# A graph convolution with experts on one core: three more batches give four columns to TensorE, deviations run ahead of block counts, and VectorE turns the experts' tiles

## The chip, the cores and the metric

The kernel runs on one core of a Trainium2 chip. Five engines run their own instruction streams and meet through semaphores: TensorE (PE, matrix products), VectorE (DVE), ScalarE (ACT), GpSimd (POOL, here mostly indirect transfers) and SyncE (SP, which issues most other transfers). The metric is the device time of one execution in microseconds; the time before is the median of three runs, 3089.98 us (3088.39 to 3091.4).

## The reference

Two graph-attention convolutions (GAT) over 6250 nodes and 206250 edges, self-loops included, then a layer of eight experts of which each node uses two. Cut to what matters:

```python
def _gat_conv(x, W, att_src, att_dst, bias, src, dst):      # 8 heads of 16 channels
    xw = (x @ W).reshape(N, H, CPH)
    a_s, a_d = (xw * att_src).sum(-1), (xw * att_dst).sum(-1)
    e = leaky_relu(a_s[src] + a_d[dst], 0.2)
    p = exp(e - segment_max(e, dst)[dst])
    alpha = p / segment_sum(p, dst)[dst]
    return segment_sum(xw[src] * alpha[:, :, None], dst).reshape(N, H * CPH) + bias

def gnn(x, edge_index, ...):
    h0 = _gat_conv(x, W0, ..., row, col)
    h1 = _gat_conv(x, W1, ..., row[col], col[col])          # and the loops
    return _layernorm(concat([h0, h1], -1) + x) * gamma + beta

def ffn(x, Wg, bg, W1, b1, W2, b2):
    top_w, top_i = top_k(x @ Wg + bg, 2)                    # softmax over the two
    return sum(w_e * (gelu(x @ W1[e] + b1[e]) @ W2[e] + b2[e] for e of 8))

x = x + gnn(_layernorm(x), ...)
out = x + ffn(_layernorm(x), ...)
```

## The kernel before

The edges are sorted by target. The program goes through four stages.

The prologue (to about 237 us) loads the nodes in 49 tiles of 128 (NT), in seven groups of seven (GRP). VectorE takes the layer norm's statistics, ScalarE the deviations (`deviation(g)`, L988), VectorE normalises (`scales`, `normalise`, from L1469), TensorE multiplies each tile with both W, and ScalarE copies the products out (`rows(t)`, L998); SP stores them as rows of tables in memory (L613), between 26 stores of 496 KB that clear another array (L607). At the same time the first edge of each node is searched: ScalarE compares block starts (`search_signs`), GpSimd fetches one block of targets per tile by an indirect transfer (`fetch_blocks(n)`, L834, seven per group), and ScalarE counts in it (`within(t)`, L1006). A block's buffer is used again 14 blocks later, so a fetch of groups 2 and up waits for a count (`block_counted`). ScalarE's order is written out: seven counts `within(0)` to `within(6)`, then `deviation(0)`, then steps t in which `rows(t)` stands with the counts that `counted_at(t)` lists. GpSimd then scatters scores into the array that was cleared (`scatter_scores`, L842) and gathers the rows of the first 49 edge columns.

The batch stage (to about 2006 us) goes over 51 batches of up to 31 columns of 128 chunks of edges. GpSimd fetches each column's rows with one indirect gather (`gather(b)`, L881, L886), into one of three slots; it waits for an index list and for the stores of the batch that had the slot three batches before. VectorE (`scan_batch`, from L1685) and ScalarE compute attention weights and running sums along the chunks, and SP stores them (L665). In batches PE0 to 49 four columns (PEC) are not gathered: TensorE picks their rows by one-hot products with a table that VectorE and ScalarE have split in parts (`split_table`, from batch SPLIT_AT on). For these, codes of the columns' sources are computed (`code_columns`), stored to memory by one transfer (L710) and read back for each batch (`fetch_codes`, L650). All index lists, codes and stores go through the one queue of SP, in program order. In the first batches VectorE and ScalarE also normalise the nodes again, a group per batch in batches 1 to 7 (`normalise_again`, L1130; `add_biases`, L1924), through one buffer `norm_again`, and SP stores the group (L697, L698). The sums that continue from one chunk to the next are corrected in two rounds: `run_maxima`, `run_sums`, `fix_maxima`, `fix_sums` on VectorE, `carry_exps`, `fix_exps` on ScalarE, and on GpSimd an indirect fetch and an indirect store of rows (L895, L901).

A third stage combines both convolutions per node and computes the router's choice. Each node's normalised row, with its number, its two weights and its first expert behind it (260 words), is scattered to `placed` in the order of experts.

The expert stage (about 2303 to 3078 us) goes over 105 tiles of 128 rows (SLOTS). SP loads a tile from a row number that it reads from `reg` (`tile_after`, L794, L799). TensorE turns it in two transposes (`turn`, L1390, L1392) into PSUM, VectorE copies it to `xsT` (`turned`, L2177). TensorE multiplies it with the expert's W1 (`up`, L1395, L1401), ScalarE applies gelu (L1247), TensorE multiplies with W2 (`down`, L1405, L1407). VectorE copies the expert's W1 in two halves to `w1_cur` (`take_weights`, L2187), each once TensorE has used the half before; it computes the rows' weights (`weights_of`, L2193 to L2201) and weighs the answer (L2228, L2230), and GpSimd adds it to `out` by an indirect transfer (L960). Tiles use two buffers. The load of tile t + 2 is issued when the tile t + 1 has been turned and the row weights of tile t are computed (`row_ids_copied`).

## Time and profile before

| | us |
|---|---|
| median of three runs | 3089.98 (3088.39 to 3091.4) |
| the profiled execution | 3084.84 |
| its span | 3083.1 |
| GpSimd busy in the span | 1897.6 (62%) |
| TensorE busy | 2068.2 (67%) |
| VectorE busy | 2168.5 (70%) |
| ScalarE busy | 1588.3 (52%) |
| first batch's first gather to the last one's end | 236.6 to 2005.8 |

The busy shares are means over stages with different limits, so no engine looks like the bound in them. The profile is read stage by stage: by the chain of work that ended last, by the costliest groups of instructions with the idle time ahead of them and what ended it, by the busy times of a stretch, and by the timelines of single engines, where a number in brackets is the idle time before an instruction and behind it what it waited for. "issue" there is time in which the engine waited for nothing that the profile shows.

### The profile page before, as it was taken

How to read it: one execution, taken by the hardware profiler on the slowest of the kernel's cores; microseconds unless marked ns; L12 is line 12 of the kernel's file. 1: busy time of each engine (PE TensorE's matmuls, PEld its weight loads, DVE VectorE, ACT ScalarE, POOL GpSimd, SP SyncE). 2: the span in 40 equal slices, each digit the busy share in tenths (PEclk: the TensorE clock that was granted, in tenths of full speed). 3: DMA queues.
4: the chain of work that ended last, by engine and by line, in shares of the span. 5: the costliest groups of instructions: out<-in, count | busy, mean ns of one | idle time of the engine just before them, and what ended most of it. 6: DMA issues, size and time to landing. Idle time of an engine off the chain costs nothing.

```text
span 3083.1 us, 41470 instructions
## 1 busy us (share of the span) xinstructions
PE 2068.2 (67%) x11476; PEld 1955.4 (63%) x11477; DVE 2168.5 (70%) x4427; ACT 1588.3 (52%) x2552; POOL 1897.6 (62%) x1880
## 2 busy tenths in 40 slices
PE   3800000058888788788878878503549999999998
PEld 1500000058888788788878878503439999999997
DVE  5668767678788878878888887888844444444443
ACT  4523333267777777777777777524423333333332
POOL 4777777777777777777777777777762222222222
PEclk9855555579899898989989898855559999999999
DMA  9445459944444444444444444475672222222222
GB/s 343 131 123 145 169 168 204 155 124 126 139 147 126 126 160 126 126 138 148 126 126 160 126 126 140 138 247 185 228 242 35 36 36 38 36 36 38 36 36 31
DMA packets 216756, 394.75 MB, mean 128 GB/s; under 512 B 80877, under 2 KB 169266, under 8 KB 210146
## 3 DMA queue, kind: packets, MB, share of 16 engines
q1 hardware_dynamic: 141169, 247.04, 24.1%
q0 software_dynamic: 74384, 146.42, 21.2%
q10 hardware_dynamic: 1120, 0.52, 0.1%
q14 instruction: 71, 0.57, 0.1%
q8 instruction: 12, 0.20, 0.0%
HBM read 202.05 MB, written 191.79 MB: 128 GB/s over the span
## 4 chain that ended last, share of the span: by engine, by line
POOL 46%; PE 26%; issue 16%; DVE 6%; DMA 2%; SPq 2%; ACT 1%; DVEq 1%; POOLq 0%; ACTq 0%
POOL AR L886 43%; PE ps L1401 12%; PE ps L1407 12%; DMA tables<-AR 1%; PE ps L1274 1%; POOL room L923 1%; PE ps L1392 1%; DVE group_stats L1968 1%; ACT AR L1207 1%; SPq L607 1%; DVE AR L1672 1%; POOL placed L951 1%; SPq L591 1%; POOL adstart L846 0%; DVE AR L2092 0%
## 5 line engine op out<-in xcount | busy, mean ns | idle before, releaser
L886 POOL DMA_INDIRECT AR<-tables,idx x1403 | 1336.9, 953 | 429.6 <-issue 427.3
L1303 PE MATMUL ps<-table_parts,onehot 128*128 128x408 f32 (+1 forms) x4080 | 881.3, 379 | 322.0 <-DVE AR L1784 164.2
L1303 PEld LDWEIGHTS ps<-table_parts,onehot 128*128 128x128 f32 x4080 | 836.3, 215 | 353.8 <-ACT onehot L1163 192.4
L1088 ACT COPY AR<-AR 128x1984 f32<-128x1984 f32 (+3 forms) x110 | 401.5, 3650 | 353.1 <-DVE AR L1719 310.4
L960 POOL DMA_INDIRECT out<-AR,idb x105 | 185.3, 1765 | 592.3 <-issue 558.3
L1719 DVE TENSOR_TENSOR_SCAN AR<-ps,AR 128x512 f32<-128x512 f32 x404 | 454.1, 1195 | 0.0
L1401 PEld LDWEIGHTS ps<-AR 128*128 128x128 f32 x3360 | 393.2, 193 | 6.6 <-DVE AR L2187 1.3
L1401 PE MATMUL ps<-AR 128*128 128x128 f32 x3360 | 393.8, 276 | 0.9 <-DVE AR L2187 0.9
L1712 DVE TENSOR_TENSOR AR<-AR,ps 128x3968 f32<-128x3968 f32 (+1 forms) x51 | 356.4, 6988 | 0.0
L2187 DVE COPY AR<-AR 128x1024 f32 x210 | 151.6, 722 | 208.2 <-PE ps L1401 206.7
L1303 PE MATMUL ps<-table_parts,onehot_dve 128*128 128x408 f32 (+1 forms) x1360 | 272.3, 343 | 0.0
L1247 ACT ACTIVATE AR<-ps,bcur 128x128 f32<-128x128 f32 x424 | 121.1, 369 | 258.5 <-PE ps L1401 258.5
L1163 ACT ACTIVATE onehot<-onehot 128x1536 fp32r<-128x1536 f32 (+1 forms) x160 | 250.6, 1566 | 5.1
L1247 ACT ACTIVATE room<-ps,bcur 128x128 f32<-128x128 f32 x416 | 118.9, 368 | 253.6 <-PE ps L1401 253.4
L1303 PEld LDWEIGHTS ps<-table_parts,onehot_dve 128*128 128x128 f32 x1360 | 246.8, 188 | 0.2
L1691 DVE TENSOR_TENSOR AR<-AR,ps 128x248 f32<-128x248 f32 (+1 forms) x51 | 29.4, 576 | 232.5 <-DMA AR<-tables,idx 232.5
L1407 PE MATMUL ps<-AR 128*128 x848 | 191.9, 379 | 1.3 <-DVE AR L2230 1.3
L1335 PE MATMUL ps<-ident,sml 128*128 128x128 f32 x6 | 2.4, 501 | 281.2 <-DVE sml L1866 281.2
L1407 PE MATMUL ps<-AR,room 128*128 x832 | 188.2, 379 | 0.0
L1159 ACT ACTIVATE onehot<-AR,minus_code 128x384 fp32r<-128x384 f16 x340 | 180.6, 609 | 5.0 <-DVE table_parts L1809 5.0
L1335 PEld LDWEIGHTS ps<-ident,sml 128*128 128x128 f32 x6 | 1.5, 312 | 282.1 <-DVE sml L1866 282.1
L1159 ACT ACTIVATE onehot<-room,minus_code 128x384 fp32r<-128x384 f16 x340 | 180.4, 605 | 0.0
(350 smaller groups left out, 2808.4 us busy)
## 6 DMA issues: line engine op xcount, KB each, us to landing
state<-AR SPq DMA_DIRECT2D x50, 2232.0 KB, 9.6
AR<-tables,idx POOLq DMA_INDIRECT x1452
AR<-in_L_ffn_W SPq DMA_DIRECT2D x16, 1024.0 KB, 10.0
AR<-placed SPq DMA_DIRECT2D x105, 130.0 KB, 2.1
adstart<-room SPq DMA_DIRECT2D x26, 496.0 KB, 13.6
AR<-adstart SPq DMA_DIRECT2D x50, 248.0 KB, 4.0
tables<-AR SPq DMA_DIRECT2D x49, 136.0 KB, 2.2
room<-tables SPq DMA_DIRECT2D x14, 476.0 KB, 4.6
```

The source lines that it names most:

```text
L886: pool.indirect_dma_start(out=G[s][:, j, 0:ROWT], out_offset=None, in_=table_rows, in_offset=bass.IndirectOffsetOnAxis(ap=idx[:, s, j:j + ...
L960: pool.indirect_dma_start(out=out, out_offset=bass.IndirectOffsetOnAxis(ap=idb[:, s, :], axis=0), in_=ys[:, s, :], in_offset=None, bounds_ ...
L1088: return S.copy(to.rearrange("p j (h c) -> p j h c", h=HD)[:, :, :, a:z], of[:, :, 1:n + 1].rearrange("p (c h) j -> p j h c", h=HD)[:, :, ...
L1159: last = S.activation(onehot[:, a, :], column_codes[b % 2][:, 0:ACT_C * P], ACT.Abs, bias=minus_code[:, v:v + 1])
L1163: S.activation(onehot[:, first:end, :], onehot[:, first:end, :], ACT.Relu, bias=1.0, scale=-1.0).then_inc(marked_by_act, 1)
L1247: last = S.activation(hsT[s][:, m, :], ps[2 * s + h][:, (m % 4) * P:(m % 4 + 1) * P], ACT.Gelu, bias=bcur[:, s, m:m + 1])
L1303: return T.matmul(bank[:, 0:z], mark, table_parts[:, k, v * w:v * w + z], start=(a == 0 and k == 0), stop=(a == LEV - 1 and k == PARTS - 1))
L1401: mm = T.matmul(ps[2 * s + h][:, m * P:(m + 1) * P], w1_cur[:, k, (h * 4 + m) * P:(h * 4 + m + 1) * P], xsT[:, s, k, :], start=(k == 0), s ...
L1407: mm = T.matmul(ps[5][:, 0:D], hsT[s][:, m, :], AR[:, bass.ds(e * (MH * D) + (NEX * KD * HID + m * D), D)], start=(m == 0), stop=(m == MH ...
L1712: V.tensor_tensor(TS[:, 0:F, js].rearrange("p (c h) j -> p c h j", h=HD), rows_in[:, :, 0:F].rearrange("p j (h c) -> p c h j", h=HD), bc(W ...
L1719: V.tensor_tensor_scan(T2[:, i * step:(i + 1) * step], decays(w), T2[:, i * step:(i + 1) * step], 0.0, ALU.mult, ALU.add).then_inc(entry_u ...
L2187: V.tensor_copy(w1_cur[:, :, h * 512:(h + 1) * 512], w1s[:, bass.ds(e, 1), :, h * 512:(h + 1) * 512].rearrange("p a k h -> p (a k) h")).th ...
```

## The change

Three things change.

First, PE0 goes from 10 to 7: batches 7, 8 and 9 gather 27 columns instead of 31, and TensorE picks four in each. What has to be ready for it moves to earlier batches: the table's load (TABLE_AT 5 to 4) and split (SPLIT_AT 8 to 5), the columns' codes (`code_columns` from the end of batch 5 to the start of batch 2, their store in SP's order from batch 6 to batch 3), the normalising of seven groups (NORMS, now in batches 1 to 4, two groups in each of the first three, through two buffers), and both rounds of corrected sums with their fetches and stores on GpSimd (batches 3, 5, 7 and 9 to 2, 3, 4 and 6).

Second, ScalarE's `deviation(0)` runs ahead of the first seven block counts, and `counted_at` spreads those counts over the steps t.

Third, a tile of the experts is turned by VectorE. Its transpose works in blocks of 32 x 32, so the tile is loaded by four transfers of 32 partitions x 4 x 64 words, which put each block where the transpose leaves it in the right place, and a fifth transfer for the last four words of each row (`row_ends`). The order of the 256 inputs in `xsT` is another one, and W1 is loaded in the same order, in four transfers instead of one for each expert. TensorE's two transposes and VectorE's copy out of PSUM go. In `one_answer`, `turned` now stands ahead of `take_weights`, and waits for the tile's load.

The diff, cut to its core:

```diff
-FIX = 5
+FIX = 2
...
-PEEL = 8
+NORMS = {1: (0, 1), 2: (2, 3), 3: (4, 5), 4: (6,)}
+PEEL = 5
...
-PE0, PE1 = 10, NB - 1
-TABLE_AT = 5
-SPLIT_AT = 8
+PE0, PE1 = 7, NB - 1
+TABLE_AT = 4
+SPLIT_AT = 5
...
-FIX_B = 7
+FIX_FETCH, FIX_STORE = (2, 4), (3, 6)
+QUAD = 32
+QUADS = P // QUAD
+TILE_LOADS = 16 * (QUADS + 1)
...
+        def counted_by(t):
+
+            return min(2 * t if t <= 4 else 8 + 3 * (t - 4) // 2, NT)
+
         def counted_at(t):
 
-            return [b for b in range(GRP + 3 * (t - 1) // 2, GRP + 3 * t // 2) if b < NT] if t >= 1 else []
+            return list(range(counted_by(t - 1), counted_by(t))) if t >= 1 else []
...
                 for b in range(NB):
-                    if 1 <= b < PEEL:
-                        g = b - 1
+                    for g in NORMS.get(b, ()):
                         sp.wait_ge(biased_ready, 2 * (g + 1))
-                        sp.dma_start(hbd[g], norm_again.rearrange("p t d -> p (t d)")).then_inc(biased_stored, 16)
+                        sp.dma_start(hbd[g], norm_again[g % 2].rearrange("p t d -> p (t d)")).then_inc(biased_stored, 16)
...
                 def up_in(e):
-                    sp.dma_start(w1s[:, e, :, :], eW1[e].rearrange("(k p) h -> p k h", p=P)).then_inc(expert_weights_loaded, 16)
+                    for q in range(QUADS):
+                        sp.dma_start(w1s[q * QUAD:(q + 1) * QUAD, e, :, :],
+                                     eW1[e][q * KD * QUAD:(q + 1) * KD * QUAD, :].rearrange("(k p) h -> p k h", p=QUAD)).then_inc(expert_weights_loaded, 16)
...
+                def load_tile(s, first):
+
+                    for q in range(QUADS):
+                        sp.dma_start(xs[q * QUAD:(q + 1) * QUAD, s, :].rearrange("p (b f) -> p b f", b=QUADS),
+                                     placed[bass.ds(first, P), q * KD * QUAD:(q + 1) * KD * QUAD].rearrange("(b p) f -> p b f", p=QUAD)).then_inc(tile_loaded[s], 16)
+                    sp.dma_start(row_ends[:, s, :], placed[bass.ds(first, P), D:ROWP]).then_inc(tile_loaded[s], 16)
...
                     r = place_row(i * 2 + (s + 2))
-                    hold(sp, 0, tile_turned, i * 2 + (s + 1))
+                    hold(sp, 0, tile_turned_copied, i * 2 + (s + 1))
                     hold(sp, 0, row_ids_copied, i * 2 + (s + 1))
-                    sp.dma_start(xs[:, s, :], placed[bass.ds(r, P), :]).then_inc(tile_loaded[s], 16)
+                    load_tile(s, r)
...
-            for b in range(GRP):
-                within(b)
             deviation(0)
...
-            def turn(s):
-                for k in range(KD):
-                    mm = T.transpose(ps[4][:, k * P:(k + 1) * P], xs[:, s, k * P:(k + 1) * P], ident[:, :])
-                mm.then_inc(tile_turned, 1)
...
-                if exists(t + 2):
-                    pe.wait_ge(tile_loaded[s], i * 16 + 32)
-                    turn(s)
                 pe.wait_ge(gelu_ready, i * 2 + (s + 1))
...
             for b in range(1, NB):
-                if b < PEEL:
-                    add_biases(b - 1)
+                if b == 2:
+                    run_sums(0)
+                    code_columns()
+                if b == 3:
+                    fix_sums(0)
+                    spread_lasts(1)
+                if b == 4:
+                    run_sums(1)
+                    V.tensor_copy(run_end, chunk_run[:, :, P])
+                if b == 5:
+                    fix_sums(1)
+                    V.tensor_copy(chunk_run[:, :, 0], run_end)
+                    dd()
+                for g in NORMS.get(b, ()):
+                    add_biases(g)
...
-            def turned(s, value):
-
-                dve.wait_ge(tile_turned, value)
-                V.tensor_copy(xsT[:, s, :, :], ps[4][:, 0:D].rearrange("p (k t) -> p k t", k=KD)).then_inc(tile_turned_copied, 1)
+            def turned(s, pairs):
+
+                dve.wait_ge(tile_loaded[s], pairs * TILE_LOADS)
+                V.transpose(xsT[:, s, :, :].rearrange("p k (b t) -> p b k t", t=QUAD), xs[:, s, :].rearrange("p (b k t) -> p b k t", b=QUADS, k=KD)).then_inc(tile_turned_copied, 1)
...
                     e = expert_of(i * 2 + (s + 2))
+                    turned(s, i + 2)
                     for h in range(2):
                         hold(dve, 4, hidden_half_ready, i * 4 + (2 * s + h + 3))
                         take_weights(h, e)
-                    turned(s, t + 3)
                     hold(dve, 4, gelu_ready, t + 1)
                     take_bias(s, e)
```

How instructions stand now, at three places. In the names, AR is the large working array in SBUF, ps is PSUM, and a bracket gives the semaphores that an instruction waits for.

ScalarE in the prologue, before: L1004 copies a tile's row out, L1009 counts in a block, whose buffer (of 14) stands in the bracket, here blocks 30 to 33.

```order
L1009 ACTIVATE AR,node_count<-AR,nidh 128x275 [waits block_gathered2]
L1016 ACTIVATE AR,node_count<-AR,nidh 128x750 [waits searched_by_act]
L996 COPY room<-ps 128x256 [waits projected,norm_turned]
L1004 COPY AR<-ps 128x304 [waits row_kept,row_stored3,projected]
L1009 ACTIVATE AR,node_count<-AR,nidh 128x275 [waits block_gathered3]
L996 COPY room<-ps 128x256 [waits projected,norm_turned]
L1004 COPY AR<-ps 128x304 [waits row_kept,row_stored0,projected]
L1009 ACTIVATE AR,node_count<-AR,nidh 128x275 [waits block_gathered4]
L1009 ACTIVATE AR,node_count<-AR,nidh 128x275 [waits block_gathered5]
```

After, at the same rows of the tables (L1022 copies the row, L1027 counts):

```order
L1027 ACTIVATE AR,node_count<-AR,nidh 128x275 [waits block_gathered11]
L1034 ACTIVATE AR,node_count<-AR,nidh 128x750 [waits searched_by_act]
L1014 COPY room<-ps 128x256 [waits projected,norm_turned]
L1022 COPY AR<-ps 128x304 [waits row_kept,row_stored3,projected]
L1027 ACTIVATE AR,node_count<-AR,nidh 128x275 [waits block_gathered12]
L1014 COPY room<-ps 128x256 [waits projected,norm_turned]
L1022 COPY AR<-ps 128x304 [waits row_kept,row_stored0,projected]
L1027 ACTIVATE AR,node_count<-AR,nidh 128x275 [waits block_gathered13]
L1027 ACTIVATE AR,node_count<-AR,nidh 128x275 [waits block_gathered0]
```

Behind the same rows stand blocks 25 to 28 now: each count is five blocks later in this order.

VectorE in the loop over the experts' tiles, before: L2187 copies a half of W1, L2180 the turned tile, L2191 the bias, and L2183 reads the expert's number ahead of the row weights.

```order
L2187 ISA [waits hidden_half_ready]
L2187 COPY AR<-AR 128x2x512
L357 REGISTER_ALU
L2187 ISA [waits hidden_half_ready]
L2187 COPY AR<-AR 128x2x512
L2179 REGISTER_ALU
L2180 COPY AR<-ps 128x256 [waits tile_turned]
L2191 ISA [waits gelu_ready]
L2191 COPY bcur<-eb1T 128x8
L357 ISA
L2183 TENSOR_LOAD reg [waits tile_loaded_a]
```

After (L2183 is the transpose now, L2190 the copy of a half of W1, L2194 the bias):

```order
L2183 STREAM_TRANSPOSE AR<-AR 128x4x2x32 [waits tile_loaded_a]
L361 ISA
L2190 ISA [waits hidden_half_ready]
L2190 COPY AR<-AR 128x2x512
L361 REGISTER_ALU
L2190 ISA [waits hidden_half_ready]
L2190 COPY AR<-AR 128x2x512
L361 REGISTER_ALU
L2194 ISA [waits gelu_ready]
L2194 COPY bcur<-eb1T 128x8
L361 ISA
L2186 ISA [waits tile_loaded_b]
```

The turning of the tile moved ahead of both halves, and with it the wait for the tile's load.

SP in the loop over the tiles, before: one load per tile.

```order
L789 TENSOR_LOAD reg
L789 ISA x2
L357 REGISTER_ALU
L799 ISA [waits tile_turned,row_ids_copied]
L799 DMA AR<-placed 128x260
```

After:

```order
L361 REGISTER_ALU
L805 ISA [waits tile_turned_copied,row_ids_copied]
L805 DMA AR<-placed 32x4x64
L805 ISA
L805 DMA AR<-placed 32x4x64
L805 ISA
L805 DMA AR<-placed 32x4x64
L805 ISA
L805 DMA AR<-placed 32x4x64
L807 ISA
L807 DMA AR<-placed 128x4
```

Where one transfer stood behind the wait, there are five, and the wait is for the turned copy instead of the turning.

## Rows read from the trace of the kernel before

**Rows 1.** The page's chain that ended last, its shares by line.

```profile
POOL AR L886 43%; PE ps L1401 12%; PE ps L1407 12%; DMA tables<-AR 1%; PE ps L1274 1%; POOL room L923 1%; PE ps L1392 1%; DVE group_stats L1968 1%; ACT AR L1207 1%; SPq L607 1%; DVE AR L1672 1%; POOL placed L951 1%; SPq L591 1%; POOL adstart L846 0%; DVE AR L2092 0%
```

**Rows 2.** The page's costliest groups: line, operation, count | busy us, mean ns | idle before.

```profile
L886 POOL DMA_INDIRECT AR<-tables,idx x1403 | 1336.9, 953 | 429.6 <-issue 427.3
...
L1691 DVE TENSOR_TENSOR AR<-AR,ps 128x248 f32<-128x248 f32 (+1 forms) x51 | 29.4, 576 | 232.5 <-DMA AR<-tables,idx 232.5
```

**Rows 3.** Busy us by stretch: POOL alone in one batch, all engines among experts.

```profile
core 0: us, POOL busy (x), PEclk, DMA share, GB/s
742.60:776.30 33.70, 25.49 (x27) 0.90 0.43 135
...
core 0: us, PE busy (x) PEld busy (x) DVE busy (x) ACT busy (x) POOL busy (x), PEclk, DMA share, GB/s
2500.00:2600.00 100.00, 100.00 (x691) 94.27 (x690) 47.43 (x168) 31.24 (x111) 23.17 (x15) 1.00 0.24 37
```

**Rows 4.** Line L2230, 2400 to 3000: count, ns min/median/max, first and last start.

```profile
L2230 DVE TENSOR_SCALAR AR<-AR,wb x83: 352/353/355, 2402.4 to 2996.5; 128x256 f32<-128x256 f32 x83
```

**Rows 5.** POOL's timeline: start, duration us, line, operation [idle before <- what ended it].

```profile
476.16 0.97 POOL L886 DMA_INDIRECT AR<-tables,idx  x1 [0.30 <-issue]
...
598.30 0.94 POOL L886 DMA_INDIRECT AR<-tables,idx  x1 [0.30 <-issue]
...
639.98 1.01 POOL L901 DMA_INDIRECT state<-fix_row,fix_index  x1 [0.30 <-issue]
```

**Rows 6.** Lines L1135 and L1927, the normalising: ns min/median/max.

```profile
L1135 ACT ACTIVATE room<-AR,nmr,rstd x49: 583/584/627, 306.1 to 547.0; 128x256 f32<-128x256 f32 x49
...
L1927 DVE TENSOR_TENSOR room<-room,ps x7: 2020/2022/2023, 309.7 to 547.6; 128x1792 f32<-128x1792 f32 x7
```

**Rows 7.** Timelines of VectorE and of SP's queue around the codes' store.

```profile
398.80 0.57 DVE L1691 TENSOR_TENSOR AR<-AR,ps 128x248 f32<-128x248 f32 x1 [5.80 <-DMA AR<-tables,idx]
...
423.95 0.32 SPq L647 DMA_DIRECT2D idx<-srcp  x1
...
515.36 0.95 SPq L710 DMA_DIRECT2D codes<-room  x1
544.19 24.09 SPq L647 DMA_DIRECT2D idx<-srcp  x1
...
567.57 0.57 DVE L1691 TENSOR_TENSOR AR<-AR,ps 128x248 f32<-128x248 f32 x1 [14.29 <-DMA AR<-tables,idx]
```

**Rows 8.** Timelines of SP's queue and of ScalarE in the prologue.

```profile
44.64 1.03 SPq L613 DMA_DIRECT2D tables<-AR  x1
...
61.26 0.41 ACT L1004 COPY AR<-ps 128x304 f32<-128x304 f32 x1 [4.77 <-issue]
```

**Rows 9.** Timelines of POOL and ScalarE at the end of the sixth fetch.

```profile
95.09 0.95 POOL L839 DMA_INDIRECT AR<-in_dst,node_index  x1 [0.30 <-ACT AR L1009]
96.34 1.01 POOL L846 DMA_INDIRECT adstart<-room,node_index  x1 [0.30 <-issue]
...
98.25 0.53 ACT L1009 ACTIVATE AR<-AR,nidh 128x275 f32<-128x275 int32 x1
```

**Rows 10.** PE's timeline in the loop over the experts' tiles.

```profile
2608.01 0.38 PE L1392 MATMUL ps<-ident,AR 128*128 128x128 f32 x2
2608.22 3.62 PE L1407 MATMUL ps<-AR 128*128 x16
```

**Rows 11.** VectorE's timeline in the same loop, one tile.

```profile
2608.41 0.69 DVE L2187 COPY AR<-AR 128x1024 f32 x1 [0.89 <-PE ps L1401]
2609.03 0.42 DVE L2180 COPY AR<-ps 128x256 f32<-128x256 f32 x1
2609.36 0.16 DVE L2191 COPY bcur<-eb1T 128x8 f32 x1
...
2610.28 0.21 DVE L2199 SCALAR_TENSOR_TENSOR both_w<-AR,expert_now 128x1 f32<-128x1 f32 x1
```

**Rows 12.** SP's queue in the same loop: the load of a tile.

```profile
2610.72 0.34 SPq L799 DMA_DIRECT2D AR<-placed  x1
```

**Rows 13.** Line L622, three index lists issued back to back: ns, and landing us.

```profile
L622 SPq DMA_DIRECT2D idx<-srcp x3: 432/433/455, 137.6 to 138.6; - x3
...
DMA to landing us min/median/max: 1.8/1.9/1.9
```

**Rows 14.** The page's transfers: line, count, KB each, median us to landing.

```profile
AR<-placed SPq DMA_DIRECT2D x105, 130.0 KB, 2.1
```

More of the change, by code:

```diff
@@ L102 @@
 STRETCHES = ((0, 5), (5, 9), (9, 13), (13, 17))
-FIX_B = 7
-assert SLOTS % 2 == 1 and FIX_B + 1 < PE0 - 1
+FIX_FETCH, FIX_STORE = (2, 4), (3, 6)
+QUAD = 32
+QUADS = P // QUAD
+TILE_LOADS = 16 * (QUADS + 1)
+WEIGHT_LOADS = 16 * (QUADS + 1)
+assert SLOTS % 2 == 1 and SPLIT_AT == PEEL and FIX + 2 <= PE0 - 3
 assert NBLK * BLK == E and NG * GRP == NT and (NB + NA) % NS == 1 and sum(CO) == J1 and max(CO) * 2 * ROWS <= J * ROWS
@@ L363, in at_tile @@
             return slice(t, t + 1) if isinstance(t, int) else bass.ds(t, 1)
+        def counted_by(t):
+            return min(2 * t if t <= 4 else 8 + 3 * (t - 4) // 2, NT)
         def counted_at(t):
-            return [b for b in range(GRP + 3 * (t - 1) // 2, GRP + 3 * t // 2) if b < NT] if t >= 1 else []
+            return list(range(counted_by(t - 1), counted_by(t))) if t >= 1 else []
         def count_step(g):
-            return g * GRP + 5
+            return g * GRP + (6 if g < NG - 1 else 5)
         def act_searches(t):
@@ L381, in build @@
         for g in range(NG):
-            assert any(GRP * (g + 1) - 1 in counted_at(t) for t in range(count_step(g))) or g == 0
+            assert any(GRP * (g + 1) - 1 in counted_at(t) for t in range(count_step(g)))
         def by_pe(b):
@@ L450, in build @@
         assert 1024 + GRP * HJ + RB * WR <= 4880 and 3 * C + NBLK <= KO
-        norm_again = eb2b.rearrange("p e d -> p (e d)")[:, 0:GRP * D].rearrange("p (t d) -> p t d", d=D)
+        norm_again = [a[:, 0:GRP * D].rearrange("p (t d) -> p t d", d=D) for a in (eb2b.rearrange("p e d -> p (e d)"), own_pair.rearrange("p s t r -> p (s t r)"))]
         bias_spread = ps[7][:, D:2 * D]
@@ L562, in build @@
         at = 2 * NEX * KD * HID
-        xs = AR[:, at:at + 2 * ROWP].rearrange("p (s d) -> p s d", s=2)
-        at += 2 * ROWP
+        xs = AR[:, at:at + 2 * D].rearrange("p (s d) -> p s d", s=2)
+        at += 2 * D
+        row_ends = AR[:, at:at + 2 * (ROWP - D)].rearrange("p (s d) -> p s d", s=2)
+        at += 2 * (ROWP - D)
         xsT = AR[:, at:at + 2 * D].rearrange("p (s k t) -> p s k t", s=2, k=KD)
@@ L905, in _ @@
                 gather(b)
-                for n, of in enumerate((3, FIX_B)):
-                    if b == of:
+                for n in range(2):
+                    if b == FIX_FETCH[n]:
                         gather_fix_rows(n)
-                    if b == of + 2:
+                    if b == FIX_STORE[n]:
                         store_fix_rows(n)
@@ L1130, in normalise_again @@
             def normalise_again(g):
-                if g >= 1:
-                    act.wait_ge(biased_stored, 16 * g)
+                if g >= 2:
+                    act.wait_ge(biased_stored, 16 * (g - g % 2))
                 for t in range(GRP):
                     n = g * GRP + t
-                    last = S.activation(norm_again[:, t, :], X[:, n, :], ACT.Identity, bias=nmr[:, n:n + 1], scale=rstd[:, n:n + 1])
+                    last = S.activation(norm_again[g % 2][:, t, :], X[:, n, :], ACT.Identity, bias=nmr[:, n:n + 1], scale=rstd[:, n:n + 1])
                 last.then_inc(norm_again_ready, 1)
@@ L1177, in whole_batch @@
                     mark_stretch(b + 2, 1)
-                if b in (1, FIX_B - 2):
+                if b in (1, 3):
                     carry_exps(0 if b == 1 else 1)
-                if b in (3, FIX_B):
-                    fix_exps(0 if b == 3 else 1)
+                if b in (2, 4):
+                    fix_exps(0 if b == 2 else 1)
             for b in range(NB - 1):
@@ L1933, in _ @@
             for b in range(1, NB):
-                if b < PEEL:
-                    add_biases(b - 1)
+                if b == 2:
[11 more added lines that the diff above has]
+                    dd()
+                for g in NORMS.get(b, ()):
+                    add_biases(g)
                 if b == PEEL:
```

47 lines of the change are left out of this document (13 added, 34 removed).

## The prediction

> **What bounds the kernel now.** I read the page's chain by line first, then its costliest groups, the busy times by stretch, and the timelines of the engines that wait. The chain is led by GpSimd's gathers, 43%, and by the experts' matrix products, 12% and 12% [rows 1]: two stages with different limits. In the batch stage GpSimd is never late: 1403 gathers of 953 ns, and 427.3 us of idle time that is only its own issue, 0.305 us each, while VectorE waits for gathers 232.5 us in 49 times, 4.7 each [rows 2]. A batch of 27 gathers takes 33.70 us, so a gather is 1.248 us of the path [rows 3]. In the expert stage TensorE is busy 100.00 of 100.00 us at granted clock 1.00, VectorE 47, GpSimd 23 [rows 3]; a tile takes (2996.5 - 2402.4)/82 = 7.245 us [rows 4]. The profiled execution took 3084.84 us (span 3083.1), 5.1 less than the median of 3089.98; the sum is made on the former, and 5.1 is added.
>
> **The gathers.** Batches 7, 8 and 9 lose four gathers each: 12. At 1.248 us that is 15.0, all on the path, since nothing else holds GpSimd there. The other end is the pace of batch 9, (639.98 - 598.30)/31 = 1.345, 16.1 in all [rows 5]; its slow gathers go with the splitting of the table, which happens as often after the change. I take -15.0.
>
> What moves ahead for it must be in time. The extra group of normalising in batches 1 to 3 costs ScalarE 7 x 0.584 = 4.1 us and VectorE 2 x 2.02 = 4.0 [rows 6]; VectorE's wait of 4.7 (5.80 in batch 3 [rows 7]) hides it, and where it doesn't quite, GpSimd, whose slots come back three batches later, does not see it. GpSimd's four transfers for the links between chunks keep their number and come in batches 2, 3, 4 and 6. The first store, which waits for VectorE's corrected sums with all later gathers queued behind it, falls behind batch 3, near 394; VectorE had done that batch's work ahead of the gathers by 398.80 - 5.80 = 393.0 [rows 7], and the sums stand first in it. On the sync queue the codes' store (L710) goes out at 515.36, and the fetch of an index list behind it stands 24.09 us from 544.19, so that VectorE waits 14.29 us for gathers [rows 7]; GpSimd had run on, and made it up. The change issues that store three batches earlier. The stall then hits the fetch that goes out at 423.95: with the same 515.36 to 568.28 = 53 us from the store to the end of the stall, a twelfth more for 172 columns than for 160, and a store near 398, it ends near 455, and the list lands some ten us later, against GpSimd's need of it at 476.16 [rows 5]. The cover is about 10 us; were it gone, every us more would be a us of the path. I count 0.
>
> **The prologue.** ScalarE's first deviations run ahead of seven block counts, so VectorE's first normalised tiles come sooner. But the table rows leave on a queue full of clears: a store goes out at 44.64, and ScalarE's next row starts only at 61.26, after 4.77 us of waiting [rows 8]. I expect this gate to stay and to eat the gain ahead of it. What stays is that a block is counted five places later in ScalarE's order (the first order rows: block 27, slot 13, stands where block 32, slot 4, stood). GpSimd's sixth fetch waits gather by gather for the counts of blocks 21 to 27. Its last gather started at 95.09, the scatters 0.30 us behind it [rows 9]. Block 27 is now counted where the count at 98.25 + 0.53 ran [rows 9], so with its read-out that gather starts near 99.1: 4.0 us later, and GpSimd, idle for issue alone from there on, has no gap to take it up. Bounds: -2, should the rows come forward too, and +6, an allowance of 2 for counts that slip further. I take +4.0, since landings set ScalarE's times there and the change does not move them.
>
> **The experts.** Removed are two TensorE transposes per tile: they start at 2608.01 and the next products at 2608.22 [rows 10], 0.21 us, which leaves 7.245 - 0.21 = 7.03 per tile, at most -22 over 103 tiles. Removed too is VectorE's copy out of PSUM, 0.42, of which 0.33 is pitch [rows 11]; added is a VectorE transpose of the same 128x256, which the trace does not show. Its nearest rows are the 0.353 us of a 128x256 multiplication [rows 4] and this copy; as bounds I take 0.35 and twice the copy, 0.8, and as value 0.4, by the copy, which has the same elements in and out. VectorE has room for it, but its order changes: the transpose stands ahead of the weight copies and waits for the tile's load. Queued behind that wait are both halves of W1, the bias and the row weights; TensorE's next tile waits for the halves. This closes a loop: the end of the row weights lets SP start the next load, and the load lets VectorE go on.
>
> Its length C, from one end of L2199 to the next: SP starts 2610.72 - 2610.49 = 0.23 us behind it [rows 11, 12]. It now issues five transfers instead of one. Back to back the queue's issues take 0.433 us and, with a gap of some 0.05, 0.48 [rows 13], so the fifth starts 1.9 later, or 2.1 with 0.05 more each for the loop's registers. A load lands in 1.9 to 2.1 [rows 13, 14]: 4.0 to 4.4 behind the end of L2199. Then 0.1 of start, the transpose 0.4, the first half 0.62 (2609.03 - 2608.41), and from the second half's start to the end of L2199 2610.49 - 2608.41 less the 0.33 of the copy, 1.75 [rows 11]. C is 6.9 to 7.3 so; 6.8 with the transpose at 0.35, and 7.7 with it at 0.8. It straddles TensorE's 7.03. I take 7.08: (7.08 - 7.245) x 103 = -17, between -22 and, at 7.7, +47.
>
> The Trainium skill, DMA: Bandwidth & Descriptors, section Bandwidth, speaks against this edit: transfers under 64 KB are dominated by their descriptors, it rules, and the tile's one load of 130 KB is cut into four of 32 KB and one of 2 KB. By it the landing, not the issue, would grow, and C would stand near the long end, for a sum of +36 instead of -27. The rows bear out only that size hardly sets the time of one load, 1.9 against 2.1 [rows 13, 14].
>
> The Trainium skill, VectorE: DVE Perf Modes, section The three transpose paths, gives 311 ns for VectorE's 128x128 of a 2-byte type, and the page's rules leave such a tile to TensorE. By its figure the two of a tile are 0.62 us, an estimate, C is 7.3 and the sum -5. No run here shows the operation.
>
> Around the loop: the first tile's five loads start the stage some 2 us later, less about 1.5 that TensorE's turning of it took; the 24 more issues for W1 in four parts, about 0.48 each, lie in SP's idle time before the router's end. Together +0.5, from 0 to +3.
>
> **The sum.** -15.0 + 4.0 - 17 + 0.5 = -27.5: 3057.3 in the profiled execution, 3062.4 as a median.
>
> **Rivals.**
> 1. The loads stay hidden and the prologue gives nothing back: -15 - 22 = -37, a median of 3053. For it: C's lower rows; against: the counts in question have no earlier place.
> 2. The tile-load loop becomes the bound, slower than now. At C = 7.6 the stage gains (7.6 - 7.245) x 103 = +37, in all +26, 3116; at 7.7, +36, 3126. It decides from where it eats the other terms' -10.5, C = 7.245 + 0.10 = 7.35, and is slower by over 0.2% from 7.41; from 7.29 to 7.41 nothing is to be measured. For it: five transfers on one queue, one tile of cover, and a wait ahead of the copies; against: the rows' sum of 6.9 to 7.3, and a DMA share of 0.24 [rows 3].
> 3. GpSimd meets the codes' stall: the list lands 20 us later than counted, 10 beyond its cover: +10, 3072. For it: that store held a fetch for 24 us; against: the margin above.
> 4. The columns do not help: the split, late by the same stall, makes TensorE late in batches 7 to 9, and GpSimd waits for a slot as long as it had gained: +15, 3077. Against: slots are reused three batches on, some 30 us.
>
> **How the numbers follow.** 0.2% is 6.2 us, about what a measurement of this kernel can tell from no change. The forecast has 0.47 (0.03 of it within 0.2%, by C near 7.3), rival 1 0.18, rival 2 0.18 (0.13 slower, 0.05 within), rival 3 0.10 and rival 4 0.07 (0.03 of both within). Faster 0.44 + 0.18 + 0.14 = 0.76, same 0.11, slower 0.13. The range leaves out rival 2's slower part, 0.13, and 0.05 for a gain beyond the best ends of gathers, prologue and experts together, -16 - 2 - 22 = -40: 3050 to 3091.
>
> **What would show it.** Right: 1391 gathers, with idle time that is issue alone, and four columns on TensorE from batch 7; the last gather of the sixth fetch near 99, and the first batch's gathers about 4 us later; tiles 7.03 to 7.15 apart, TensorE waiting at most 0.1 per tile for weight copies. Wrong: tiles over 7.3 apart, with VectorE's transpose waiting for the load in each; GpSimd waiting for an index list near 477; first gathers no later than before; a VectorE transpose near 0.8 us.

## The result, and the profile after

The changed kernel takes 3056.77 us (median of four runs, 3055.04 to 3057.26) beside 3090.03 for the kernel before: a ratio of 0.9891, 95% interval 0.9878 to 0.9903, or 33.3 us less. The forecast was 3062.4 with a range of 3050 to 3091. The profiled execution took 3056.33 us with a span of 3054.5, 28.6 less than the span before.

Where the 28.6 us come from, read from both traces by the first and the last gather of the batches, TensorE's first product for a tile, and the end:

| stretch | before | after | difference | forecast |
|---|---|---|---|---|
| start to the first batch's first gather | 236.6 | 239.1 | +2.5 | +4.0 |
| first gather to the end of the last | 1769.3 | 1758.0 | -11.2 | -15.0 |
| from there to TensorE's first product for a tile | 302.7 | 304.5 | +1.8 | +0.5 |
| from there to the end | 774.6 | 752.9 | -21.7 | -17 |

The rows behind these, of the changed kernel. First the page's costliest groups, which answer [rows 2]:

```profile
L904 POOL DMA_INDIRECT AR<-tables,idx x1391 | 1328.0, 955 | 425.9 <-issue 423.6
...
L1695 DVE TENSOR_TENSOR AR<-AR,ps 128x248 f32<-128x248 f32 (+1 forms) x51 | 29.4, 577 | 215.2 <-DMA AR<-tables,idx 215.1
...
L2183 DVE STREAM_TRANSPOSE AR<-AR 128x256 f32<-128x256 f32 x105 | 46.8, 446 | 176.9 <-DMA AR<-placed 176.9
```

Twelve gathers are gone and GpSimd is still idle for issue alone, so no list and no slot kept it waiting. But one gather takes 955 ns where it took 953: some of what the 12 saved is lost again in longer ones. VectorE's new transpose takes 0.446 us and waits for the tile's load in every one of its 105 runs.

The timelines of GpSimd, ScalarE and SP's queue at the places of [rows 7 to 9]: start and duration in us, line, operation, and the idle time ahead with what ended it.

```profile
63.14 0.41 ACT L1022 COPY AR<-ps 128x304 f32<-128x304 f32 x1 [17.11 <-issue]
...
94.89 0.95 POOL L857 DMA_INDIRECT AR<-in_dst,node_index  x1 [1.22 <-ACT AR L1027]
...
98.86 0.94 POOL L857 DMA_INDIRECT AR<-in_dst,node_index  x1 [0.52 <-DVE room L1482]
...
239.08 0.94 POOL L904 DMA_INDIRECT AR<-tables,idx  x1 [2.28 <-DMA state<-AR]
...
401.40 1.29 SPq L719 DMA_DIRECT2D codes<-room  x1
439.71 14.70 SPq L657 DMA_DIRECT2D idx<-srcp  x1
```

ScalarE's first rows come sooner and it then idles 17.11 us, where it idled 4.77, for the same gate: its next row starts at 63.14 (61.26 before). GpSimd's sixth fetch now waits for counts within the group and its last gather starts at 98.86 (95.09). For that gather the profile names a VectorE copy (L1482), but in the code it waits for a count of ScalarE's alone. The codes' store stalls the fetch behind it until 454.4, and batch 6's gathers start at 484.8 without waiting.

The loop over the tiles: the busy times of the engines in 100 us, columns as in [rows 3].

```profile
2500.00:2600.00 100.00, 100.00 (x689) 94.22 (x689) 48.25 (x170) 33.08 (x116) 24.13 (x15) 1.00 0.29 37
```

And the line that weighs the answers, once per tile, between 2400 and 2980: count, ns min/median/max, first and last start.

```profile
L2233 DVE TENSOR_SCALAR AR<-AR,wb x83: 352/353/355, 2400.7 to 2976.9; 128x256 f32<-128x256 f32 x83
```

Tiles are (2976.9 - 2400.7)/82 = 7.027 us apart, and TensorE, at granted clock 1.00, has no gap: it is the bound as before, with the 0.21 us of its two transposes taken off in full.

### The profile page after: what moved, and what is told of

It is laid out like the page before. It is cut to its first block, busy times and chain, and to the rows that moved or that the text cites. A ratio compares the mean times of both kernels' runs of the same rounds, so it can differ in the third digit from the quotient of the medians.

```text
span 3054.5 us, 43131 instructions
## 1 busy us (share of the span) xinstructions
PE 2130.1 (70%) x11674; PEld 2016.2 (66%) x11675; DVE 2185.0 (72%) x4466; ACT 1632.3 (53%) x2615; POOL 1877.3 (61%) x1868
## 4 chain that ended last, share of the span: by engine, by line
POOL 46%; PE 26%; issue 16%; DVE 6%; SPq 2%; DMA 1%; ACT 1%; DVEq 1%; POOLq 0%; ACTq 0%
POOL AR L904 43%; PE ps L1412 12%; PE ps L1418 12%; PE ps L1290 1%; POOL room L941 1%; SPq L617 1%; DVE group_stats L1971 1%; ACT AR L1223 1%; DMA tables<-AR 1%; SPq L601 1%; DVE AR L1676 1%; POOL placed L969 1%; POOL adstart L864 0%; DVE AR L2095 0%; DVE AR L2092 0%
## 5 line engine op out<-in xcount | busy, mean ns | idle before, releaser
L1319 PE MATMUL ps<-table_parts,onehot 128*128 128x408 f32 (+1 forms) x4386 | 950.9, 380 | 327.0 <-DVE AR L1788 176.8
L1319 PEld LDWEIGHTS ps<-table_parts,onehot 128*128 128x128 f32 x4386 | 902.4, 216 | 361.1 <-ACT onehot L1179 203.2
L978 POOL DMA_INDIRECT out<-AR,idb x105 | 174.2, 1659 | 581.8 <-issue 546.7
L1412 PEld LDWEIGHTS ps<-AR 128*128 128x128 f32 x3360 | 394.3, 193 | 34.2 <-issue 29.0
L1319 PE MATMUL ps<-table_parts,onehot_dve 128*128 128x408 f32 (+1 forms) x1462 | 292.7, 343 | 0.0
L1179 ACT ACTIVATE onehot<-onehot 128x1536 fp32r<-128x1536 f32 (+1 forms) x172 | 269.3, 1566 | 5.5
L1319 PEld LDWEIGHTS ps<-table_parts,onehot_dve 128*128 128x128 f32 x1462 | 265.3, 188 | 0.2
L1175 ACT ACTIVATE onehot<-room,minus_code 128x384 fp32r<-128x384 f16 x374 | 198.5, 607 | 3.4 <-DVE table_parts L1813 3.4
L2183 DVE STREAM_TRANSPOSE AR<-AR 128x256 f32<-128x256 f32 x105 | 46.8, 446 | 176.9 <-DMA AR<-placed 176.9
L1418 PEld LDWEIGHTS ps<-AR 128*128 128x128 f32 x848 | 157.1, 190 | 20.8 <-issue 1.7
```

What stands on the lines that cost most here:

```text
L978: pool.indirect_dma_start(out=out, out_offset=bass.IndirectOffsetOnAxis(ap=idb[:, s, :], axis=0), in_=ys[:, s, :], in_offset=None, bounds_ ...
L1175: last = S.activation(onehot[:, a, :], column_codes[b % 2][:, 0:ACT_C * P], ACT.Abs, bias=minus_code[:, v:v + 1])
L1179: S.activation(onehot[:, first:end, :], onehot[:, first:end, :], ACT.Relu, bias=1.0, scale=-1.0).then_inc(marked_by_act, 1)
L1319: return T.matmul(bank[:, 0:z], mark, table_parts[:, k, v * w:v * w + z], start=(a == 0 and k == 0), stop=(a == LEV - 1 and k == PARTS - 1))
L1412: mm = T.matmul(ps[2 * s + h][:, m * P:(m + 1) * P], w1_cur[:, k, (h * 4 + m) * P:(h * 4 + m + 1) * P], xsT[:, s, k, :], start=(k == 0), s ...
L1418: mm = T.matmul(ps[5][:, 0:D], hsT[s][:, m, :], AR[:, bass.ds(e * (MH * D) + (NEX * KD * HID + m * D), D)], start=(m == 0), stop=(m == MH ...
```

## The experiments

**One part at a time.** Three kernels make one of the three changes each to the kernel before, and a fourth is the changed kernel without the first of them. `p1_prologue_only` is this:

```diff
-            return [b for b in range(GRP + 3 * (t - 1) // 2, GRP + 3 * t // 2) if b < NT] if t >= 1 else []
+            return list(range(counted_by(t - 1), counted_by(t))) if t >= 1 else []
...
-            for b in range(GRP):
-                within(b)
             deviation(0)
```

> The kernel before with ScalarE's new order alone (deviation(0) ahead of the seven block counts, counts spread over the steps). Theory, the sum of separate parts: the last gather of GpSimd's sixth fetch comes near 99 instead of 95.1, the first batch's first gather 2.5 to 4 us after 236.6, and the whole time is longer by that: +2.5 to +4 us, ratio 1.0008 to 1.0013. Rival: the order itself costs nothing and the later start of the changed kernel comes from its other parts: first gather at 236.6, ratio 1.000.

3092.02 us beside 3089.5: ratio 1.0007 (0.9998 to 1.0016), +2.5 us, an interval that still holds no difference, so the time alone decides nothing. The trace has the mechanism: GpSimd's sixth fetch ends in waits for ScalarE's counts, its last gather at 97.39 instead of 95.09, and the first batch starts at 239.32.

```profile
93.42 0.95 POOL L843 DMA_INDIRECT AR<-in_dst,node_index  x1 [1.32 <-ACT AR L1013]
...
97.39 0.95 POOL L843 DMA_INDIRECT AR<-in_dst,node_index  x1 [0.52 <-ACT AR L1013]
...
239.32 0.95 POOL L890 DMA_INDIRECT AR<-tables,idx  x1 [2.04 <-DMA state<-AR]
```

`p2_columns_only` is the part of the batches, with all that was moved ahead for it (cut to the constants):

```diff
-FIX = 5
+FIX = 2
...
-PEEL = 8
+NORMS = {1: (0, 1), 2: (2, 3), 3: (4, 5), 4: (6,)}
+PEEL = 5
...
-PE0, PE1 = 10, NB - 1
+PE0, PE1 = 7, NB - 1
```

> The kernel before with four columns on TensorE from batch 7 and all that was moved ahead for it, alone. Theory: 12 gathers less are -15.0 us, of which 3.8 are lost again to longer gathers and a longer fetch of the link rows while VectorE adds biases to two groups in one batch: -11 us, ratio 0.9964, first batch's gather to last batch's end 1758. Rival: those longer gathers belong to the shift by the prologue and are absent here: -15 us, 0.9951, 1754.

3075.64 us: ratio 0.9953 (0.9939 to 0.9966), -13.9 us. The interval holds the theory's 11 and the rival's 15. In its trace, as in the changed kernel's, there are long gathers beside the additions of two groups, and the fetch of the second round of link rows takes 2.67 us instead of 0.94, so the rival's reason, that these come from the prologue, falls: its first batch starts at 235.7.

`p3_experts_only` has the transpose on VectorE, the five loads and W1 in quarters:

```diff
-                    sp.dma_start(xs[:, s, :], placed[bass.ds(r, P), :]).then_inc(tile_loaded[s], 16)
+                    load_tile(s, r)
...
+                    turned(s, i + 2)
...
-                    turned(s, t + 3)
```

> The kernel before with VectorE's transpose and the five loads per tile alone. Theory: TensorE stays the bound, tiles 7.03 apart instead of 7.245, -22 us less up to 1 at the stage's start: -21 to -22, ratio 0.993. Rival, the term as the prediction had it: the load's loop binds at 7.08, -17 us, 0.9945.

3067.84 us: ratio 0.993 (0.9916 to 0.9943), -21.7 us, as the theory had it. The tiles are 7.027 us apart, where the rival needs 7.08.

```profile
L2232 DVE TENSOR_SCALAR AR<-AR,wb x83: 353/354/355, 2401.4 to 2977.6; 128x256 f32<-128x256 f32 x83
```

`p4_no_prologue` is the changed kernel with the counts of ScalarE where they were:

```diff
-            return list(range(counted_by(t - 1), counted_by(t))) if t >= 1 else []
+            return [b for b in range(GRP + 3 * (t - 1) // 2, GRP + 3 * t // 2) if b < NT] if t >= 1 else []
...
             for t in range(GRP, 2 * GRP):
                 search_signs(t)
+            for b in range(GRP):
+                within(b)
             deviation(0)
```

> The changed kernel with ScalarE's former order in the prologue, the other two parts as they are. Theory: it gains what that order cost, 2.5 to 4 us under the changed kernel, 36 us under the kernel before, ratio 0.988; first gather at 236.6. Rival: the parts are not separate, and the earlier deviations are needed for the rest to be in time: same as or slower than the changed kernel, ratio 0.989 or more.

3052.91 us: ratio 0.9883 (0.9868 to 0.9898) to the kernel before, 3.9 us under the changed kernel's 3056.77. The first gather is at 236.12. These two medians come from different occasions, and against its own runs of the kernel before each gains 36.6 and 33.3, 3.3 apart, with intervals that overlap. With p1's +2.5 and the first gathers of the traces (239.08 and 236.12 here, 239.32 and 236.6 in p1 and the kernel before) it says the same: the new order in the prologue costs 2.5 to 4 us. The parts add up, +2.5 - 13.9 - 21.7 = -33.1 beside the measured -33.3, closer than intervals of 3 to 4 us either way on each part would lead one to expect.

**What lengthens the gathers.** In the changed kernel's trace VectorE adds to two groups in a row, and GpSimd's gathers beside it are long. VectorE first, then GpSimd, the changed kernel:

```profile
312.25 2.02 DVE L1931 TENSOR_TENSOR room<-room,ps 128x1792 f32<-128x1792 f32 x1 [1.30 <-ACT room L1151]
314.19 2.02 DVE L1932 TENSOR_TENSOR AR<-AR,bet 128x1792 f32<-128x1792 f32 x1
316.12 2.01 DVE L1931 TENSOR_TENSOR room<-room,ps 128x1792 f32<-128x1792 f32 x1
318.06 2.02 DVE L1932 TENSOR_TENSOR AR<-AR,bet 128x1792 f32<-128x1792 f32 x1
...
315.29 1.74 POOL L904 DMA_INDIRECT AR<-tables,idx  x1 [0.30 <-issue]
317.33 0.94 POOL L904 DMA_INDIRECT AR<-tables,idx  x1 [0.30 <-issue]
318.57 2.32 POOL L904 DMA_INDIRECT AR<-tables,idx  x1 [0.30 <-issue]
...
357.98 0.94 POOL L904 DMA_INDIRECT AR<-tables,idx  x1 [0.31 <-issue]
359.22 2.31 POOL L913 DMA_INDIRECT fix_row<-state,fix_index  x1 [0.30 <-issue]
```

The two long gathers end at 317.03 and 320.89, each 0.81 or 0.82 us behind the end of an L1932 (316.21 and 320.08). The gather between them, beside an L1931, takes its usual 0.94. The kernel before has the same once per group: seven gathers of 1.62 to 2.40 us, each ending 0.81 or 0.82 behind its second addition (L1928). L1932 reads both operands from SBUF; L1931 takes one from PSUM (`ps`). `m1_beta_psum` puts that to the test, on top of p4:

```diff
-        beta_spread = bet[:, :]
+        beta_spread = ps[5][:, 0:D]
...
             V.tensor_copy(bias_spread, b01[:, :])
+            V.tensor_copy(beta_spread, bet[:, :])
```

> As p4_no_prologue, with one operand moved: the second addition of each group, X += beta (2.02 us, both operands in SBUF), reads beta from PSUM, as the first addition already does with the bias. It does the same work for as long. Theory: a VectorE instruction with both operands in SBUF holds GpSimd's gather back while both run, so that the gathers of batches 1 to 4 and the fetch of link rows lose their extra time: the gathers' time above 0.944 us each falls from 14.8 us to about 7 (what the table's splitting takes stays), the fetch from 2.31 to 0.95, and the whole is 8 to 9 us under p4_no_prologue, near 3044. Rival: it is VectorE's traffic as such, or the two groups in a row, whatever the operands: extra time 14 us or more, time as p4_no_prologue, 3053.

3042.54 us: ratio 0.9854 (0.9838 to 0.9871), 10 us under p4 (9.8 when each is set against its own runs of the kernel before). The addition still takes 2.02 us, and no gather of batches 1 to 5 is longer than 1.05.

```profile
308.95 2.02 DVE L1929 TENSOR_TENSOR room<-room,ps 128x1792 f32<-128x1792 f32 x1 [1.21 <-ACT room L1149]
310.89 2.01 DVE L1930 TENSOR_TENSOR AR<-AR,ps 128x1792 f32<-128x1792 f32 x1
312.82 2.02 DVE L1929 TENSOR_TENSOR room<-room,ps 128x1792 f32<-128x1792 f32 x1
...
310.22 0.94 POOL L900 DMA_INDIRECT AR<-tables,idx  x1 [0.30 <-issue]
311.46 0.94 POOL L900 DMA_INDIRECT AR<-tables,idx  x1 [0.30 <-issue]
312.71 0.94 POOL L900 DMA_INDIRECT AR<-tables,idx  x1 [0.30 <-issue]
```

The gathers' time above 0.944 us each falls from 14.8 to 6.9, and what is left lies in the batch that splits the table; with the link rows' fetch at 0.94 again the batch stage is 9.3 us shorter. So the operand is the cause, not the length of the addition, nor two groups in a row. The Trainium skill, SBUF — State Buffer, section SBUF: two separate sides, has this as a rule: a VectorE instruction with two SBUF inputs and a GpSimd operation that reads SBUF take one port pair in turns, each for a whole instruction. The trace agrees for these additions, where a gather ends 0.81 us behind the addition's end; that VectorE waits in its turn does not show, since L1932 takes 2.015 to 2.018 us each time. This is also the fastest kernel of the study.

`m0_before_beta_psum` makes the same edit in the kernel before:

> The kernel before with beta read from PSUM in the second addition of each group, nothing else. Question: why the kernel before was profiled 5.1 us under its median, while the changed one was profiled at its median. Theory: how long the gathers beside those additions take depends on how the two happen to meet in an execution. The profile of before was a lucky one (12.4 us above 0.944 each in all; two other kernels with the same batch stage showed 17.3 and 18.7), so with the additions out of the way about 6 stay (the table's splitting), the median falls by 11 to 12 us to about 3078, ratio 0.9963, and the 12 gathers are then worth their 15. Rival: the 5.1 us lie elsewhere in the program; the median falls only by what the profile of before shows, 12.4 - 6.1 = 6 us, to 3083, ratio 0.998.

3080.98 us: ratio 0.9976 (0.9967 to 0.9985), -7.8 us, with an interval from -4.6 to -10.2. It holds the rival's 6 and not the theory's 11, so the theory falls: the stalls of the profile before were at most some 2 us short of the usual. What I had taken for longer stalls in p1 and p3 is partly another pace of every gather. The gather's line in p1, ns min/median/max:

```profile
L890 POOL DMA_INDIRECT AR<-tables,idx x1403: 943/947/2564, 239.3 to 2014.1; - x176
```

And in m0:

```profile
L886 POOL DMA_INDIRECT AR<-tables,idx x1403: 940/944/2159, 237.4 to 2000.1; - x176
```

The median is 947 ns in p1, p2 and p3, and 944 in the kernel before, in the changed one, in p4 and m1: 3 ns x 1403 = 4.2 us. It does not follow the code of the batches, which p2 and p4 share, nor the chip alone, since p1 to p4 ran on the same one. Above its own median the gathers beside the additions cost 6.2 us in the kernel before, 8.4 in p1 and 7.7 in p3: the meeting of gather and addition does differ between these executions, by about 2 us, and the 7.8 lies in this range.

**How near the tile's load is to being the bound.** In the changed kernel's loop VectorE waits for the load, SP for VectorE. VectorE's and SP's timelines:

```profile
2602.15 0.21 DVE L2202 SCALAR_TENSOR_TENSOR both_w<-AR,expert_now 128x1 f32<-128x1 f32 x1
...
2606.29 0.45 DVE L2183 STREAM_TRANSPOSE AR<-AR 128x256 f32<-128x256 f32 x1 [1.49 <-DMA AR<-placed]
2606.66 0.66 DVE L2190 COPY AR<-AR 128x1024 f32 x1
2607.54 0.69 DVE L2190 COPY AR<-AR 128x1024 f32 x1 [0.22 <-PE ps L1412]
...
2602.59 1.82 SPq L805 DMA_DIRECT2D AR<-placed  x4
2604.60 0.35 SPq L807 DMA_DIRECT2D AR<-placed  x1
```

From the row weights' end at 2602.36 to the first issue are 0.23 us, to the fifth 2.01 more, to the transpose 1.69 more. The rest of the loop, to the next end of L2202, takes what TensorE leaves it, so it doesn't show how long the loop would be alone. `x1_six_loads` makes it longer:

```diff
                     sp.dma_start(row_ends[:, s, :], placed[bass.ds(first, P), D:ROWP]).then_inc(tile_loaded[s], 16)
+                    sp.dma_start(spare[:, s, :], placed[bass.ds(first, P), D:ROWP]).then_inc(tile_loaded[s], 16)
```

> The changed kernel with one more small load per tile (the four words behind each row a second time, to spare room), which nothing reads but the tile waits for. It lengthens the load by one issue, 0.42 us. Theory: the loop from the row weights' end through the load, the transpose and both weight copies back to it is as long as TensorE's 7.03 already, with no cover: tiles 7.4 to 7.5 apart, the whole 38 to 48 us over the changed kernel, slower than the kernel before. Rival: the load has cover, VectorE's 1.5 us of waiting for it cost nothing: tiles 7.03, time as the changed kernel, 3057.

3056.17 us, tiles (2976.7 - 2400.5)/82 = 7.027 apart: the rival. A sixth load is covered. The line that weighs the answers, then VectorE's and SP's timelines:

```profile
L2235 DVE TENSOR_SCALAR AR<-AR,wb x83: 352/354/355, 2400.5 to 2976.7; 128x256 f32<-128x256 f32 x83
...
2700.44 0.21 DVE L2204 SCALAR_TENSOR_TENSOR both_w<-AR,expert_now 128x1 f32<-128x1 f32 x1
...
2705.00 0.45 DVE L2185 STREAM_TRANSPOSE AR<-AR 128x256 f32<-128x256 f32 x1 [2.06 <-DMA AR<-placed]
...
2707.42 0.21 DVE L2204 SCALAR_TENSOR_TENSOR both_w<-AR,expert_now 128x1 f32<-128x1 f32 x1
...
2700.89 1.84 SPq L806 DMA_DIRECT2D AR<-placed  x4
...
2703.36 0.38 SPq L809 DMA_DIRECT2D AR<-placed  x1
```

Between the transpose and the next end of L2204 VectorE waits for nothing of TensorE's here, so the loop can be read: 0.24 to the first issue, 2.47 to the sixth, 1.64 to the transpose and 2.63 to the next end, 6.98, and 7.07 in the tile behind it. That is just at TensorE's 7.03. With the changed kernel's own 0.23, 2.01 and 1.69 and this 2.63 the loop of five loads is 6.56, an estimate. `x2_six_loads_late` has the sixth load and the transpose behind both weight copies:

```diff
-                    turned(s, i + 2)
                     for h in range(2):
                         hold(dve, 4, hidden_half_ready, i * 4 + (2 * s + h + 3))
                         take_weights(h, e)
+                    turned(s, i + 2)
```

> As x1_six_loads, with the transpose and its wait behind both weight copies, where the copy out of PSUM stood before. Theory: with the copies out of the loop it is some 6 us long, and the sixth load is covered: tiles 7.03 apart, 3057. Rival: the load itself is too late for TensorE, wherever VectorE waits for it: tiles as in x1_six_loads, 7.4 or more.

3061.15 us, tiles (2974.6 - 2405.5)/81 = 7.026 apart. With x1 at 7.03 this pair says nothing about the order; the 5 us between them lie ahead of the tiles. `x3_eight_loads` and `x4_eight_loads_late` repeat it with three more loads of one word each:

> The changed kernel with three more small loads per tile instead of one. With one more, the loop (row weights' end, six issues, landing, transpose, weight copies, row weights) was read as 0.24 + 2.47 + 1.64 + 2.63 = 6.98 us, just under TensorE's 7.03. Theory: that loop exists and has 0.47 us of cover in the changed kernel; two issues more, 0.45 each, make it 7.9: tiles 7.85 to 7.95 apart, 85 to 95 us over the changed kernel, 3142 to 3152. Rival: loads are fetched far enough ahead that the loop never binds: tiles 7.03, 3057.

3166.1 us, tiles (2973.4 - 2403.7)/71 = 8.02 apart. The line that weighs the answers, then VectorE's and TensorE's timelines in x3:

```profile
L2236 DVE TENSOR_SCALAR AR<-AR,wb x72: 352/353/355, 2403.7 to 2973.4; 128x256 f32<-128x256 f32 x72
...
2704.45 0.45 DVE L2186 STREAM_TRANSPOSE AR<-AR 128x256 f32<-128x256 f32 x1 [3.56 <-DMA AR<-placed]
...
2712.65 0.45 DVE L2186 STREAM_TRANSPOSE AR<-AR 128x256 f32<-128x256 f32 x1 [3.60 <-DMA AR<-placed]
...
2705.53 3.84 PE L1415 MATMUL ps<-AR 128*128 128x128 f32 x32 [0.63 <-DVE AR L2193]
...
2713.72 2.50 PE L1415 MATMUL ps<-AR 128*128 128x128 f32 x20 [0.75 <-DVE AR L2193]
```

The loop exists, and once it is longer than TensorE's work, TensorE waits for VectorE's weight copies in every tile, as rival 2 of the prediction had it, 0.1 us above what was expected of it here.

> As x3_eight_loads, with the transpose and its wait behind both weight copies. Theory: the 1.25 us of the copies leave the loop, which is then 7.9 - 1.25 = 6.65: tiles 7.03 apart, 3057 to 3062. Rival: order makes no difference, the load is late for TensorE itself: tiles 7.85 or more.

3096.28 us, tiles (2979.3 - 2404.0)/78 = 7.38 apart: 0.65 of the 1.0 us come back, not all.

```profile
L2236 DVE TENSOR_SCALAR AR<-AR,wb x79: 352/353/355, 2404.0 to 2979.3; 128x256 f32<-128x256 f32 x79
```

With the copies out of it the loop is still SP's issues, the landing, the transpose and the row weights, 7.3 us with what VectorE idles between the bias and the row weights (0.57 to 0.82, for issue), which my 6.65 left out. So both readings hold a part: the place of the wait costs 0.65 us a tile here, and the load itself the rest.

## Why the prediction was right, and where its terms were off

The direction and the range held: all of the gain is in the two stages where the prediction put it. Of the cases, the one that came is the forecast's with rival 1's loads: they stay hidden, while the prologue costs time, and 3056.8 lies between rival 1's 3053 and the forecast's 3062.4. The edits of batches and experts by themselves measure as gains; the prologue's +2.5 has an interval that holds nothing. That the sum of -27.5 is 1.1 from the profile's -28.6 is luck: its terms were off by +3.8, -1.5, -4.7 and +1.3. By its steps:

- **Gathers, -15.0 forecast, -11.2 in the profile, -13.9 (-10.5 to -18.8) alone.** 12 gathers at 1.248 us did go. The mean of 953 ns in [rows 2] beside the usual 944 already held stalls; 6.2 us of them were beside VectorE's additions. The step that failed is "its slow gathers go with the splitting of the table, which happens as often after the change" as the only price of a gather beside VectorE, and that the extra group of normalising would be hidden by VectorE's wait: its price was on GpSimd, not on VectorE. Against the profile before, 2.4 us went to longer gathers (14.9 above 0.944 each instead of 12.4) and 1.4 to the link rows' fetch (2.31 instead of 0.94). As an estimate from medians the two groups in a row cost less than these 3.8: the additions hold GpSimd for 9.8 us in p4 (to m1) and for 7.8 in the kernel before (to m0), so 2.0 of the 15 go to the two groups in a row.
- **What was moved ahead, 0.** Right. The list behind the codes' store was out of SP's stall at 454.4, where 455 was forecast, against a need of it at 484.8, later than the 476.16 that I had taken; GpSimd waited for nothing. Nothing of rivals 3 and 4 shows.
- **Prologue, +4.0, measured +2.5 in the profile and alone, 3.3 to 3.9 by leaving it out.** The gate did eat the gain ahead of it (17.11 us of idle time instead of 4.77), and the last gather of the sixth fetch came 3.8 us later (98.86, forecast 99.1). The term was too large by the scatters behind it: three took 1.29, 1.75 and 2.53 us in the profile before and about 1.0 in this one, where two fetches are long instead (1.39 and 1.67); that is 1.3 to 1.5 given back.
- **Experts, -17, measured -21.7.** The loop was forecast at 7.08 and reads 6.56 with five loads. Mis-sized were the landing with the start behind it (1.69 us from the fifth issue, forecast 2.0 to 2.2) and VectorE's part (2.63, forecast 2.77, though the transpose took 0.446 and not 0.4). TensorE's 7.03 was right, so the bound of the term, -22, became its value: the half of rival 1 that concerns the loads. That many small loads cost more than their issue, which the Trainium skill's rule in DMA: Bandwidth & Descriptors, section Bandwidth, would have led to, did not show here: from the fifth issue to the transpose were 1.69 us, where one load of 130 KB landed in 2.1 [rows 14].
- **Around the loop, +0.5, +1.8 in the profile**, inside its 0 to 3.
- **From the profile to the median, +5.1.** The sum was -27.5 and the spans differ by 28.6, but the medians by 33.3. Adding 5.1 assumed that whatever put the profiled execution below its median would be there for the changed kernel too. It was not: the changed kernel was profiled within 0.5 us of its median. GpSimd's pace differs between the profiled executions, 944 or 947 ns a gather, worth 4.2 us; the three executions profiled at 947 lie 2.2 to 4.0 us above the medians of their kernels, and those at 944 of the kernels with several runs lie at their medians or below. Whether that is the whole of the 5.1 stays open, since only profiled executions show the pace.

Of the tests that the prediction named, three came out as it said for right (1391 gathers with issue alone between them, a last fetch near 99, tiles 7.03 apart) and none as it said for wrong; the first batch started 2.5 us later and not 4.

## What to carry to other kernels

A step hidden by an engine's idle time can still have a price on another engine: look at what runs beside it, instruction by instruction, where the bound engine's own durations vary (0.94 to 2.7 us for the same gather here). When a load goes to the front of a loop, write the loop out from semaphore to semaphore with the trace's own intervals; a few dummy loads then test the cover that such a sum gives (0.47 us per tile here: one load more was covered, three were not). And make the sum on differences of spans, but don't carry the offset between a profile and a median from one kernel to another.

## What the runs showed of the hardware that was not expected

- A VectorE addition of two SBUF operands holds a GpSimd gather that starts beside it until 0.81 us behind its own end, and with one operand in PSUM it doesn't at all: 10 us of 3053 for two lines (m1 to p4), 7.8 in the kernel before.
- The table's splitting takes 6.9 us of gathers in m0 and in m1. It has a bit mask (L1810 in the changed kernel) and a copy (L1812) of one SBUF operand each, and a subtraction of two (L1813). Of the nine long gathers in the changed kernel's batch 6 five start beside a copy or a subtraction and end 0.81 or 0.82 us behind it; the other four have a mask or a copy start while they are under way and end 0.12 or 0.13 behind that. No run took the three apart. VectorE, then GpSimd, in the changed kernel:

```profile
487.98 1.08 DVE L1812 CAST table_parts<-room 128x1768 fp32r<-128x1768 f32 x1
...
492.13 1.01 DVE L1812 CAST table_parts<-room 128x1632 fp32r<-128x1632 f32 x1
493.06 1.85 DVE L1813 TENSOR_TENSOR table_parts<-room 128x1632 fp32r<-128x1632 f32 x1
...
487.31 1.87 POOL L904 DMA_INDIRECT AR<-tables,idx  x1 [0.30 <-issue]
...
492.49 1.47 POOL L904 DMA_INDIRECT AR<-tables,idx  x1 [0.30 <-issue]
494.26 1.46 POOL L904 DMA_INDIRECT AR<-tables,idx  x1 [0.30 <-issue]
```

- A VectorE transpose of 128x256 words in 32x32 blocks takes 0.446 us. The Trainium skill, VectorE: DVE Perf Modes, section The three transpose paths, has 0.311 for half as many elements of 2 bytes, so two would be an estimate of 0.62; the trace is below that.
- The same gather takes a median of 944 ns in the profiled executions of some of these kernels and 947 in others, at equal idle times between gathers (427.2 us in p1, 427.3 in the kernel before).
